# Sixteen-head attention in one transformer kernel: the clamped bias as a factor on GpSimd, norm and values on ScalarE, and a new slot table

## The reference

```python
NUM_HEADS = 16; MAX_BIAS = 8.0                   # heads of 8 columns
qkv = x @ in_proj_weight.T + in_proj_bias
rel = pos[:, None] - pos[None, :]                # query minus key
bias = jnp.minimum(rel * slopes[:, None, None], MAX_BIAS)
scores = einsum('bhqd,bhkd->bhqk', q, k) * D ** (-0.5) + bias
out = einsum('bhqk,bhkd->bhqd', softmax(scores), v)
return out @ out_proj_weight.T + out_proj_bias   # then x + this
```

## Time and profile before

| | us |
|---|---|
| three timed runs: median (lowest to highest) | 995.03 (993.92 to 995.42) |
| the profiled execution's own time | 988.53 |
| its span, first to last instruction | 986.5 |
| busy: PE / PEld / DVE / ACT / POOL | 783.2 / 564.8 / 549.3 / 395.9 / 357.9 |
| mean granted TensorE clock | 0.906 |

### The profile page before, as it was taken

How to read it: one execution, slowest core, us unless ns; L and a number is a source line. 1 busy time by engine, 2 the same in 40 slices (tenths; PEclk the granted TensorE clock), 3 DMA queues, 4 the chain that set the end, 5 groups by cost and what they waited for, 6 DMA issues and landing times.

```text
span 986.5 us, 19021 instructions
## 1 busy us (share of the span) xinstructions
PE 783.2 (79%) x5641; PEld 564.8 (57%) x5641; DVE 549.3 (56%) x2190; ACT 395.9 (40%) x947; POOL 357.9 (36%) x543
## 2 busy tenths in 40 slices
PE   0798479999999999952489999999999982038894
PEld 0676355555666677742246676667666651028883
DVE  4688573233322332333588989898987714026672
ACT  0456121222212322210036666766676661025562
POOL 5000517777850134433222423242322102744552
PEclk9999668999999999986569999999999995559997
DMA  9970001111100132303654444444443014111110
GB/s 250 155 221 0 0 1 36 40 41 41 44 0 14 52 112 78 96 30 90 128 106 95 90 108 93 102 83 106 95 85 67 3 45 155 54 53 55 50 50 14
DMA packets 75114, 72.44 MB, mean 73 GB/s; under 512 B 8125, under 2 KB 65680, under 8 KB 72732
## 3 DMA queue, kind: packets, MB, share of 16 engines
q1 hardware_dynamic: 69436, 60.38, 27.3%
q0 software_dynamic: 5600, 11.12, 3.5%
HBM read 43.71 MB, written 27.33 MB: 72 GB/s over the span
## 4 chain that ended last, share of the span: by engine, by line
PE 52%; DVE 18%; issue 12%; DMA 5%; POOL 5%; ACT 3%; DVEq 2%; SPq 2%; POOLq 0%; ACTq 0%
PE bank L1475 10%; PE bank L1476 9%; DVE rt L1065 6%; PE bank L1498 6%; PE bank L1527 4%; PE bank L1617 3%; PE bank L1569 3%; POOL sorted_rows L766 3%; PE bank L1604 3%; PE bank L1599 2%; DMA arena<-arena 2%; SPq L548 1%; DVEq L1180 1%; PE bank L1435 1%; PE bank L1707 1%
## 5 line engine op out<-in xcount | busy, mean ns | idle before, releaser
L1065 DVE CUSTOM_DVE_ANT_0 rt<-bank,alibi 128x256 f32<-128x256 f32 x512 | 192.9, 419 | 44.4 <-PE bank L1569 37.5
L973 DVE TENSOR_TENSOR arena<-arena,bank 128x512 f32<-128x512 f32 (+1 forms) x128 | 75.0, 587 | 187.8 <-ACT arena L1253 187.8
L1280 ACT ACTIVATE arena<-bank 128x512 f32<-128x512 f32 x256 | 150.6, 598 | 55.4 <-PE bank L1604 49.5
L1253 ACT ACTIVATE arena<-bank 128x512 f32<-128x512 f32 (+1 forms) x128 | 66.1, 517 | 202.9 <-PE bank L1476 202.9
L1569 PE MATMUL bank<-arena 72*128 72x256 bf16 x512 | 104.7, 289 | 26.6 <-DMA arena<-qk_parts 13.4
L1599 PE MATMUL bank<-arena 81*128 81x256 bf16 x512 | 117.0, 274 | 8.3 <-ACT arena L1280 4.7
L1475 PE MATMUL bank<-arena 128*128 128x320 f32 (+2 forms) x256 | 115.7, 534 | 7.5 <-DVE arena L973 7.5
L1476 PE MATMUL bank<-arena 128*128 128x320 f32 (+2 forms) x256 | 111.9, 519 | 0.0
L1604 PE MATMUL bank<-arena,ident_b 128*128 128x256 bf16 (+8 forms) x544 | 80.2, 243 | 0.0
L1569 PEld LDWEIGHTS bank<-arena 72*128 72x128 bf16 x512 | 39.0, 102 | 69.4 <-DVE arena L1065 42.8
L1475 PEld LDWEIGHTS bank<-arena 128*128 128x128 f32 x256 | 42.8, 193 | 53.5 <-DVE arena L973 41.1
(11 more groups left out here) (242 smaller groups left out, 1402.9 us busy)
## 6 DMA issues: line engine op xcount, KB each, us to landing
arena<-qk_parts SPq DMA_DIRECT2D x48, 192.0 KB
arena<-qk_parts SPq DMA_DIRECT2D x144, 64.0 KB
qk_parts<-arena SPq DMA_DIRECT2D x16, 384.0 KB, 2.8
back_rows<-empty_row SPq DMA_DIRECT2D x1, 4096.0 KB, 37.8
arena<-back_rows SPq DMA_DIRECT2D x16, 256.0 KB, 3.8
arena<-in_w SPq DMA_DIRECT2D x2, 2048.0 KB, 10.9
xg_rows<-empty_row SPq DMA_DIRECT2D x1, 2580.0 KB, 38.5
arena<-xg_rows SPq DMA_DIRECT2D x8, 322.5 KB, 4.0
```

The costliest lines, as they stand in the source:

```text
L973: nc.vector.tensor_tensor(out, sil[:, k, 0:out.shape[1]], bank[4 + k][:, 0:out.shape[1]], ALU.mult).then_inc(hid_done, 1)
L1065: last = nc.vector.tensor_tensor_reduce(biased[n % 2 * QT + u], bank[n % 2][:, SEQ * u:SEQ * u + SEQ], alibi[:, h, P * (1 - u):P * (1 - u) ...
L1253: nc.scalar.activation(sil[:, k, 0:width], bank[2 + k][:, 0:width], ACT.Silu).then_inc(sil_done, 1)
L1280: nc.scalar.activation(prT3[:, n % (2 * HG)].rearrange("p k t -> p (k t)"), bank[2 + n % 2][:], ACT.Exp).then_inc(exp3_done, 1)
```

## The change

The change does seven things, all in the stage of the slots.

- Strips remain for heads 0 and 1 alone (`FULL = 2`): 8 per batch. Heads 2 to 8 now take the linear bias in the contraction like the others, and GpSimd multiplies the exponentials, in place and where the cap holds, by `exp(min(8 - slope * distance, 0))` (`apply_factor`, 12 multiplications per batch). The factors are made once, before the stage. `weigh` of these heads waits for them (`factored`).
- Room for this: exponentials are kept for three groups instead of two (`PR`), values for five batches instead of four (`VRING`), and `weigh` comes three to four slots later, cut into two halves in two slots.
- `norm3` moves from VectorE to ScalarE, as `scale * x + shift`; GpSimd works out scale and shift (four small operations where there was one). VectorE's addition of `LN_EPS` goes.
- `values` moves from VectorE to ScalarE as two plain copies; the values' bias is projected once and added to the output bias, before the stage.
- The maxima's DMA is issued by ScalarE, one slot after `copy_max`, and is sent on ScalarE's queue. The maxima are turned in bank 6 instead of bank 7.
- `replicate` pairs the parts by diagonals: eight DMAs of 24, 16 and 8 partitions instead of twelve of 24 and 8, for the same bytes.
- `load_given` also waits for an earlier batch's maxima to have landed. The slot numbers are new throughout: projection of q, k and of v apart, the two halves of each norm apart, GpSimd's work in slots as well.

The core of the diff:

```diff
-FULL = 4
+FULL = 2
+PR = 3 * HG
+VRING = 5
-COMBINE_0, COMBINE_1, STATS, VARIANCE, NORM, TURN, HT, QKV, QK_COPY, VALUES = -41, -40, -39, -38, -33, -30, -29, -26, -25, -19
+COMBINE_0, COMBINE_1, STATS, VARIANCE, ROOT, NORM_0, NORM_1, OUTPUT_BIAS = -42, -41, -38, -37, -36, -34, -33, -29
+TURN, HT, QK, Q_COPY, K_COPY, PARTS_QK, VALUE, VALUES = -32, -31, -27, -26, -25, -24, -25, -21
...
-            for a in range(PARTS):
-                r = PARTS * HD * a
-                sp.dma_start(ks[r:r + PARTS * HD, c % RING], rows[1]).then_inc(qk3_in[c % RING], 16)
-                for k in range(PARTS):
-                    sp.dma_start(qs[r + HD * k:r + HD * k + HD, c % RING], rows[0, HD * a:HD * a + HD]).then_inc(qk3_in[c % RING], 16)
+            n = PARTS * HD
+            for i in range(PARTS):
+                sp.dma_start(qs[n * i:n * i + n, c % RING], rows[0]).then_inc(qk3_in[c % RING], 16)
+                left = n - HD * i
+                sp.dma_start(ks[n * i:n * i + left, c % RING], rows[1, HD * i:n]).then_inc(qk3_in[c % RING], 16)
+                if i:
+                    sp.dma_start(ks[n * i + left:n * i + n, c % RING], rows[1, 0:HD * i]).then_inc(qk3_in[c % RING], 16)
...
+        def apply_factor(n):
+            c, h = divmod(n, NH)
+            pool.wait_ge(exp3_done, n + 1)
...
+            for k in range(QT):
+                first = capped_from(h, k)
+                if first < SEQ:
+                    pr = prT3[:, n % PR, k, first:SEQ]
+                    last = nc.gpsimd.tensor_tensor(pr, pr, factor[:, h - FULL, first - P * k:SEQ - P * k], ALU.mult)
+            last.then_inc(factored, 1)
...
+        def normalise(c, u):
...
+            last = nc.scalar.activation(h3[:, c % 2, u, :], x[:, QT * c + u, :], ACT.Identity, scale=norm3[:, c % 2, u, 1:2],
+                                        bias=norm3[:, c % 2, u, 0:1])
...
+        def send_max(c):
+            wait_apart(act, (max_rows_done, c + 1))
+            act.dma_start(qs[MROW:KALL, c % RING], max_rows[0:PARTS * NH, c % 2]).then_inc(max_in[c % 2], 16)
```

More of the change, by code:

```diff
@@ L284, in _build @@
     strip_a = carve([P, sum(BIAS_PARTS[:FULL]), SEQ + P], BF16)
[L285 to L288 removed]
+    factor = carve([P, FACTORS, SEQ])
     q_row = carve([P, SEQ], BF16)
@@ L1129, in _ @@
                 norm3_variance(c)
-            if (c := batch_at(slot3, NORM)) is not None:
-                norm3(c)
-            if (c := batch_at(slot3, VALUES)) is not None:
-                values(c)
             if (c := batch_at(slot3, DIVIDE_0)) is not None:
@@ L1294, in turned, with values, copy_q @@
             nc.scalar.activation(hT3, bank[6][:, 0:SEQ], ACT.Copy).then_inc(hT3_done, 1)
-        def copy_qk(c):
+        def values(c):
+            act.wait_ge(v3_mm, c + 1)
+            if c >= VRING:
+                act.wait_ge(pv3_mm, NH // HG * (c - VRING + 1))
+            for u in range(QT):
+                last = nc.scalar.activation(v3[:, c % VRING, u, :, 0:HD],
+                                            bank[6][:, SEQ + D * u:SEQ + D * u + D].rearrange("p (h d) -> p h d", d=HD), ACT.Copy)
+            last.then_inc(v3_done, 1)
+        def copy_q(c):
             act.wait_ge(qk3_mm, c + 1)
@@ L1544, in turn, with project_qk, project_v @@
             last.then_inc(tr3, 1)
-        def project(c):
-            pe.wait_ge(hT3_done, c + 1)
+        def project_qk(c):
             if c >= 1:
                 pe.wait_ge(qk3_done, c)
+            pe.wait_ge(hT3_done, c + 1)
+            if c >= 7:
+                pe.wait_ge(lg5_done, c - 6)
+            for a in range(2):
+                last = nc.tensor.matmul(bank[7][:, SEQ * a:SEQ * a + SEQ], w3[:, D * a:D * a + D], hT3, start=True, stop=True)
+            last.then_inc(qk3_mm, 1)
+        def project_v(c):
+            if c >= 1:
                 pe.wait_ge(v3_done, c)
@@ L1552, in project @@
                 pe.wait_ge(max_rows_done, c - 2)
-            for a in range(2):
-                last = nc.tensor.matmul(bank[7][:, SEQ * a:SEQ * a + SEQ], w3[:, D * a:D * a + D], hT3, start=True, stop=True)
-            last.then_inc(qk3_mm, 1)
             for u in range(QT):
```

282 lines of the change are left out of this document (152 added, 130 removed).

## The result

The changed kernel takes 971.07 us (median of 4 runs, 966.96 to 973.34), the kernel before 995.05 us in the same comparison: ratio 0.976, 95% interval 0.973 to 0.979. It is faster, by 24 us, where 39 were forecast. Its profiled execution took 971.0 us; the one of before took 988.5. These two lie only 17.5 us apart, because the stages ahead of the slots took 451.3 us in the one and 442.9 in the other. That goes by the chip and not by the change: on one chip variants of both kernels took 443 to 445 us there, on another variants of both 450 to 452.

A forecast was written before the change was run, and what follows sets the result against it. TensorE and VectorE, coupled by two banks, were taken to bound the kernel. Gains of 34.6 us in the batches, 2 at the start and 2.4 in the tail made 39 off 995.0: 956 us, range 936 to 986.

The forecast's parts named there:

- The bound before: Steady slots of the kernel before: TensorE and VectorE coupled by two banks, whoever has the crowded slot holding the other up.
- Strips, 2.5 us off TensorE: Per batch, 26 of 34 strip matmuls go, 0.9 + 1.6 us, taking 2.5 us off TensorE.
- `weigh` in halves costs no more matmuls, 0.5 us in each of eight slots: TensorE's weighing, 1.00 us whole, was priced at 0.5 us per half, with no added matmuls.
- VectorE's 15.8: VectorE's time per batch: 18.0 us less moved norm and values, the LN_EPS addition and `combine`'s 0.97 us of stalls.
- the second rival: GpSimd's factor multiplications hold up VectorE's splitting of the maxima, 0.9 to 1.8 us per batch: 969 to 982 us, chance 0.15.
- ScalarE 15.4 to 16.5, GpSimd 13.7: Forecast load per batch in us after the moves: ScalarE up from 13.5, GpSimd up from 6.2.
- The yardstick and 17.2: Period 0.4 of the way from busiest engine's sum (16.0) to sum of dearest slots (18.2), plus 0.3: 17.2 us a batch.
- the first rival: Evened slots couple the engines less, so a batch takes 15.9 us: 937 us, chance 0.14.
- 14.4 batches: 231 slots from first turned scores to last maximum, each batch gaining 19.6 - 17.2 us: 34.6 us (7 to 53).
- So I expect 1.00 to stay: TensorE's granted clock stays at 1.00 (2.4 GHz) while its busy share falls from 97% to some 90%.
- Start 2, tail 2.4: Gains outside the steady batches: 2 us at the stage's start (0 to 5), 2.4 us of strips in the tail (0 to 3).
- The third rival: The maxima's DMA lands late, TensorE waits 2.1 us per batch, period 19.3: 987 us, chance 0.12.

The follow-up runs named there:

- the last variant above: Changed kernel with both halves of each weighing in the later slot and `combine` moved from VectorE to GpSimd: ratio 0.971 to the kernel before (0.9656 to 0.9764).

## Why the prediction was right in its sign and off in its size

*The bound before.* Right: both engines, coupled by two banks, though nearly half of the TensorE waits that it was read from (7.8 of 16.5 us) are the pauses behind `weigh`. Each relief alone brought little (strips 0.7 us a batch, norm and values nothing), and both together with the new slots 2.0. When only the strips went, VectorE came next 0.7 us below; when only the moved work went, TensorE was still there.

*Strips, 2.5 us off TensorE.* The runs show 2.1 of own work. The number of strips was right, the narrow ones are cheaper.

*"`weigh` in halves costs no more matmuls, 0.5 us in each of eight slots."* This is the term of the batch that failed. The matmuls are as many, but a half costs 0.57 and 0.1 at the switch before it: 1.4 us a batch more than I had put in, 1.0 of it due to the halving. The slots also held 0.85 us for the projections of queries, keys and values (a price that stands in the slot sums alone and not in the text), where start-to-start times give 0.86 + 0.54. These two make 2.0 of the 2.25 us between 15.2 and 17.45; the rest is spread over small ones. The check was at hand: the same sum for the kernel before was 17.7, and its start-to-start times less the waits give 18.5.

*VectorE's 15.8.* Right: 15.9 busy. `combine`'s stall went (346 ns). The splitting of the maxima beside the factors (the second rival) costs 0.07 us a batch by its casts' means, not 0.9 to 1.8. That was luck, since the timing that makes it so was not worked out: in these nine batches the subtraction (0.19 to 0.20 us) met only GpSimd's multiplication of 38 elements or its operations on two. In the last variant above it met the one of 166 elements three times, and took 0.47 us each time:

```profile
593.47 0.53 POOL L802 TENSOR_TENSOR arena<-arena 128x166 f32<-128x166 f32 x1
593.58 0.47 DVE L1099 TENSOR_TENSOR arena<-arena 128x32 f32<-128x32 f32 x1
```

It ended 0.05 us after GpSimd's. The Trainium skill, "SBUF — State Buffer", in its section on the two separate sides, has a VectorE operation with two inputs from SBUF wait out the whole of a GpSimd instruction that reads SBUF and started first. The trace agrees for the factor multiplications, and does not for operations on two elements, inside whose 0.71 us a subtraction still took 0.19.

*ScalarE 15.4 to 16.5, GpSimd 13.7.* Measured 14.1 and 12.2; the issue, 0.74 where I took 0.4, is not counted as busy, so ScalarE's 14.8 compare with my 15.4. The copies took 0.30 each (I took 0.28), the norm 0.505. The factors were 5.3 for 5.5; `parts` and roots overlapped more. The sign "ScalarE over 85% busy" was not met (79%). The second norm waited for the late root, as I had feared, by 0.3 us a batch.

*The yardstick and 17.2.* With VectorE as the busiest at 16.0 it gave 17.2. TensorE at 17.45 was the busiest, and the period was 17.5, no coupling loss on top: the even slots did what the first rival said, for another engine. Two errors of opposite sign, the smaller one hiding part of the larger: 2.4 us forecast a batch, 1.9 to 2.0 measured.

*14.4 batches.* This multiplied the steady gain over batches that did not have it, and it is the largest miss. From the first turned score to the last row maximum the forecast had 34.6 us, and 21.3 came. Nine batches gave 17.1 of 21.6; the other 5.4 gave 4.2 of 13.0. Those ahead of the nine gained 0.7 in all: TensorE was granted 0.50 up to 531 us where the kernel before had 1.00 from 512. "So I expect 1.00 to stay" was wrong there, and the run with eight more matmuls prices it at 4.3 us. Why those behind the nine gained only 3.5 stays open.

*Start 2, tail 2.4.* The start gave 3.3: the parts of batch 0 took 11.9 us from the first issue to landing, against 13.9. The Trainium skill, "DMA: Bandwidth & Descriptors", on why a DMA increments its semaphore by 16, led to an estimate of 11.1; the measurement is between. The tail, from the last row maximum to the last turned score, gave 2.1: right. Behind it 1.1 us were lost, on which the prediction had put nothing: the last `weigh` starts 2.9 us behind the last turned score, where it was 1.5, since `weigh` was moved back. No run tests whether that is the whole of it.

*The third rival's price.* By the prediction's own numbers TensorE's wait would have been 5.07 less 3.2, 1.9 us, and not 2.1.

The sum: 4.5 us of the missing gain are the batch length, 8.8 the batches at the ends of the stage, 0.3 the tail, 1.1 what lies behind it, less 1.3 at the start. That is 13.4, and 39 less 13.4 is, but for rounding, the 25.7 of the profiles.

## What to carry to other kernels

Price an engine's queue by start-to-start times, switches between tile shapes included, and check that the sum for the kernel before equals its measured period less its waits; then do the same sum for the new order. Before reading a wait as one for another engine, see whether it has the same length where nobody is named. When two engines are as close as here, a relief of one alone was worth a third of itself or nothing, and evening the slots traded work for waits. Before shortening a period, look at what must arrive from a DMA within it: here eight DMAs in place of twelve, worth 1.3 us by its issues, carried 3% of the kernel.
